# Batch 2 of each tile: probabilities turned by VectorE and reordered through DRAM in place of TensorE transposes, with a new order of all queues

## What is computed

```python
xq = q.reshape(b, s, N_KV_HEADS, N_REP, HEAD_DIM)     # 8 groups x 4 x 32
xk = k.reshape(b, t, N_KV_HEADS, HEAD_DIM)            # t = 257
xv = v.reshape(b, t, N_KV_HEADS, HEAD_DIM)
scores = einsum('bsgrd,btgd->bgrst', xq, xk) / sqrt(HEAD_DIM) + mask
probs = softmax(scores, axis=-1)
out = einsum('bgrst,btgd->bsgrd', probs, xv)

x = x + xattn(layernorm(x), ctx, ctx, 0, mask)
x = x + s4_convolution(layernorm(x), ...)
x = x + gated_experts(layernorm(x), ...)
```

## Time and profile before

| what | value |
|---|---|
| median of three timed executions | 1288.33 us (1287.66 to 1290.14) |
| the profiled execution, its own time | 1290.52 us |
| its span, first to last instruction | 1288.6 us |
| mean granted TensorE clock | 0.992 |
| TensorE busy | 1232.9 us, 96% |
| ScalarE busy | 1122.9 us, 87% |
| VectorE busy | 959.7 us, 74% |
| GpSimd busy | 825.4 us, 64% |
| DMA | 166.38 MB, share 40.9% of 16 engines for SP's queue |
| transposes of `pr` on TensorE | 2048 |

### The profile page before, as it was taken

One profiled execution on the slowest core, in us unless ns is written; L12 is line 12 of the kernel. 1 busy time (PEld: TensorE's weight loads), 2 busy tenths in 40 slices (PEclk: granted clock), 3 DMA queues, 4 the chain that ended last, 5 costly groups with the idle time before them and its releaser, 6 DMA issues.

```text
span 1288.6 us, 41515 instructions
## 1 busy us (share of the span) xinstructions
PE 1232.9 (96%) x13676; PEld 1083.1 (84%) x13676; DVE 959.7 (74%) x3424; ACT 1122.9 (87%) x3337; POOL 825.4 (64%) x1259
## 2 busy tenths in 40 slices
PE   3679999999999999999999999999999999999997
PEld 2558888888888888888888888888888888888886
DVE  6977777777777777877777777677777877877753
ACT  5889999998999999999999999989999999999841
POOL 4447676776667677666767766676777666777520
PEclk9979999999999999999999999999999999999999
DMA  7443443443344444434544433453443344444210
GB/s 237 134 127 93 151 155 122 130 133 125 119 148 152 124 130 132 129 123 141 155 122 131 147 124 118 134 154 123 131 151 123 122 128 154 132 125 132 61 60 33
DMA packets 150103, 166.38 MB, mean 129 GB/s; under 512 B 58217, under 2 KB 116082, under 8 KB 149890
## 3 DMA queue, kind: packets, MB, share of 16 engines
q1 hardware_dynamic: 149890, 163.72, 40.9%
HBM read 128.50 MB, written 34.08 MB: 126 GB/s over the span
## 4 chain that ended last, share of the span: by engine, by line
PE 76%; DVE 5%; DMA 4%; POOL 4%; ACT 4%; issue 3%; SPq 2%; DVEq 0%; ACTq 0%; POOLq 0%
PE ps_p L562 22%; PE ps_p L633 15%; PE ps_p L661 12%; PE ps_p L648 12%; PE ps_p L594 8%; PE ps_s L574 7%; ACT pr L840 2%; DMA dn<-den 2%; DMA xq<-in_x 1%; POOL lastp L1093 1%; DVE ms L1387 1%; SPq L381 1%; ACT pts L772 1%; DMA vl<-in_ctx 1%; POOL lastp L1103 1%
## 5 line engine op out<-in xcount | busy, mean ns | idle before, releaser
L840 ACT ACTIVATE pr<-ms,negmax 128x256 f32<-128x256 f32 x1024 | 512.6, 504 | 17.3 <-DVE negmax L1387 17.3
L1387 DVE CUSTOM_DVE_ANT_0 ms<-ps_s,neg_mask,last 128x256 f32<-128x256 f32 x1024 | 447.0, 473 | 7.1 <-PE ps_s L574 6.2
L772 ACT ACTIVATE pts<-ps_p 128x512 f32<-128x512 f32 x512 | 298.3, 590 | 45.8 <-PE ps_p L562 29.1
L562 PE MATMUL ps_p<-ident,pr 128*128 128x128 f32 x2048 | 296.5, 280 | 10.4 <-ACT pr L840 5.1
L562 PEld LDWEIGHTS ps_p<-ident,pr 128*128 128x128 f32 x2048 | 229.1, 142 | 48.0 <-issue 17.4
L840 ACT ACTIVATION_READ_ACCUMULATOR pr<-ms,negmax 128x1 f32 x1024 | 199.6, 195 | 0.0
L1061 POOL TENSOR_TENSOR kt<-kr,kt 128x512 fp32r<-128x512 f32 x128 | 164.9, 1288 | 24.1 <-ACT kt L772 24.1
L648 PE MATMUL ps_p<-wa_hi,ut_hi 128*128 128x288 f32 x512 | 159.6, 312 | 1.4 <-DVE ut_lo L1203 1.4
L648 PE MATMUL ps_p<-wa_lo,ut_hi 128*128 128x288 f32 x512 | 151.8, 296 | 0.0
L648 PE MATMUL ps_p<-wa_hi,ut_lo 128*128 128x288 f32 x512 | 151.7, 296 | 0.0
L1203 DVE TENSOR_TENSOR ut_lo<-ps_p,ut_hi 128x512 fp32r<-128x512 f32 x128 | 87.7, 690 | 74.8 <-ACT ut_hi L772 74.5
(11 more groups left out here) (139 smaller groups left out, 2584.6 us busy)
## 6 DMA issues: line engine op xcount, KB each, us to landing
cx<-in_ctx SPq DMA_DIRECT2D x128, 256.0 KB, 3.9
kr<-in_keys SPq DMA_DIRECT2D x128, 256.0 KB, 3.0
xq<-in_x SPq DMA_DIRECT2D x32, 512.0 KB, 4.3
turn_q<-xq SPq DMA_DIRECT2D x32, 512.0 KB, 2.9
qx<-turn_q SPq DMA_DIRECT2D x128, 128.0 KB, 2.9
xr<-in_x SPq DMA_DIRECT2D x32, 512.0 KB, 3.9
out_x<-tmp SPq DMA_DIRECT2D x32, 512.0 KB, 3.2
dn<-den SPq DMA_DIRECT2D x512, 2.0 KB, 2.3
```

What stands on the lines that cost most here:

```text
L562: mm = pe.transpose(into[:, j * P:(j + 1) * P], source, ident[:, :])
L772: return act.activation(out, in_, ACT.Copy, scale=scale)
L840: act.activation(pr[:, b % 2, g, :], ms[:, n % MS, :], ACT.Exp, bias=negmax[:, n % MS:n % MS + 1], scale=-1.0, accum_out=den[:, b, g:g + 1 ...
L1387: dve.tensor_tensor_reduce(ms[:, n % MS, :], ps_s[:, g % GPH, g // GPH * SW:(g // GPH + 1) * SW], neg_mask[:, 0:SW], 1.0, last[:, it % 2, ...
```

## The change

For batch 2 of every tile (`TURNED = (2,)`), TensorE's transposes and ScalarE's copies go. In their place:

- `exp` writes the four groups of a half of `pr` interleaved, so that element (group g, key j * 128 + i * 32 + t) stands at column ((i * 2 + j) * 4 + g) * 32 + t.
- `p_turn` (VectorE, twice for each tile, after `maximum` 23 and after `maximum` 29 and the first `q_turn`) turns half of `pr` in place, 128x1024, in 32x32 blocks: afterwards partition (r, t) holds, for each (i, j, g), the 32 positions.
- `store_p` (SP, twice) writes such a half, 512 KB, to `turn_p` in DRAM, 4 KB from each partition.
- `load_p` (SP, twice) waits for the store of its half and reads it back: partition t * 4 + i, for each r a run of 1 KB, into `pts`, 512 KB.
- `attend` for batch 2 reads its moving operand from there, as four runs of 32 columns, 512 elements apart, and waits for `p_loaded`, not for `pair_copy`.
- The host lays the context rows out as `values`, so that `load_context` brings one run of 2 KB to each partition for all batches, and for batch 2 in the key order t * 4 + i that the loaded probabilities have.
- `exp` of a batch that reuses a half of `pr` waits for `p_stored` where the one before was batch 2, and for `pt_done` otherwise, now once for each half.
- The lists of all five engines and the table `BANKS` are written anew. In the SP list of an iteration the two stores stand first, then `turn_last`, the two loads, `load_context(it - 1, 2)`, `load_residual(it - 1)`, `move_den(it - 1, 2)` and `(it - 1, 3)`.

```diff
-PAIRS = STEPS // 2
+TURNED = (2,)
+def paired(m):
+    return sum(k // GPH not in TURNED for k in range(m))
+PAIRS = paired(STEPS // 2)
+            def store_p(it, k, h):
+                sp.wait_ge(p_turned[k][h], at(it, 1, 1))
+                if at(it, 16, 0) > 0:
+                    sp.wait_ge(p_loaded[k][h], at(it, 16, 0))
+                sp.dma_start(turn_p[k, h, :, :, :],
+                             pr[:, TURNED[k] % 2, GPH * h:GPH * (h + 1), :]).then_inc(p_stored[k][h], 16)
+            def load_p(it, k, h):
+                b = TURNED[k]
+                sp.wait_ge(p_stored[k][h], at(it, 16, 16))
+                if at(it, 2 * BPT, 2 * b - 2) > 0:
+                    sp.wait_ge(pv_done, at(it, 2 * BPT, 2 * b - 2))
+                sp.dma_start(pts[:, b % 2 * GPH:(b % 2 + 1) * GPH, h * SW:(h + 1) * SW],
+                             turn_p[k, h, :, :, :].rearrange("(r t) i c -> (t i) r c", r=REP)).then_inc(p_loaded[k][h], 16)
             def attend(it, hh):
-                pe.wait_ge(pc_done, at(it, PAIRS, 2 * hh + 2))
+                if b in TURNED:
+                    pe.wait_ge(p_loaded[TURNED.index(b)][h], at(it, 16, 16))
+                else:
+                    pe.wait_ge(pc_done, at(it, PAIRS, paired(2 * hh + 2)))
+                turned = pts[:, b % 2 * GPH:(b % 2 + 1) * GPH, :].rearrange("p r (h j q s) -> p h j q r s", h=HALVES, j=TBLK, q=GPH)
...
+            def p_turn(it, k, h):
+                b = TURNED[k]
+                dve.wait_ge(e_done, at(it, STEPS, GROUPS * b + GPH * (h + 1)))
+                half = pr[:, b % 2, GPH * h:GPH * (h + 1), :].rearrange("p g c -> p (g c)")
+                dve.transpose(half, half).then_inc(p_turned[k][h], 1)
```

More of the change, by code:

```diff
@@ L67 @@
 BANKS = {
[L68 to L71, removed]
+    "pair": (1, 0, 0, 2, 0, 2, 0, 2, 2, 0, 3, 3, 0, 3, 1, 3,),
+    "out": (1, 0,),
+    "u": (0, 1,),
+    "z": (3, 1,),
     "g": (1,),
-    "y": (2, 3,),
+    "y": (0, 1,),
     "f": (3, 2,),
-    "b": (1, 0,),
+    "b": (1, 2,),
     "o": (3, 2, 3, 1,),
-    "keys": (0,),
+    "keys": (2,),
     "router": (2,),
[L79 to L83, removed]
+    "sums": (2,),
+    "dft": (3,),
+    "rows": (1,),
+    "strip": (3, 1, 2,),
+    "w": (1, 1, 2, 0, 2, 3, 2, 1, 0, 1, 3, 1, 0, 2, 3, 3,),
 }
@@ new lines, in _ @@
+            pair_chunk(31, 0); pair_chunk(31, 1); attend(30, 4); attend(30, 5); scores(31, 1); attend(30, 6)
+            attend(30, 7); pair_chunk(31, 2); experts(29, 0, 0, 1); experts(29, 0, 1, 3); experts(29, 0, 3, 5)
+            out_chunk(30, 0); out_chunk(30, 1); experts(29, 0, 5, 6); experts(29, 0, 6, 8); pair_chunk(31, 3)
+            pair_chunk(31, 4); gated_chunk(29); scores(31, 2); attend(31, 0); attend(31, 1); pair_chunk(31, 5)
+            pair_chunk(31, 6); expand(29, 0, 0, 4); expand(29, 1, 0, 2); expand(29, 1, 2, 3); expand(29, 1, 3, 4)
@@ new lines, in _ @@
+            u_chunk(30, 0); scores(31, 3); pair_chunk(31, 7); u_chunk(30, 1); convolve(30, 0, 0, 4)
+            convolve(30, 1, 0, 1); convolve(30, 1, 1, 8); z_chunk(30, 0, 0); attend(31, 2); z_chunk(30, 1, 0)
+            attend(31, 3); pair_chunk(31, 12); pair_chunk(31, 13); pair_chunk(31, 14); experts(30, 1, 0, 1)
+            experts(30, 1, 1, 3); pair_chunk(31, 15); experts(30, 1, 3, 4); experts(30, 1, 4, 6); experts(30, 1, 6, 8)
+            attend(31, 4); attend(31, 5); attend(31, 6); attend(31, 7); experts(30, 0, 0, 1); experts(30, 0, 1, 3)
@@ new lines, in _ @@
+            q_stats(2, 2); q_turn(1, 1); maximum(0, 24); weight_low(4, 1); maximum(0, 25); p_turn(0, 0, 1)
+            maximum(0, 26); maximum(0, 27); maximum(0, 28); maximum(0, 29); maximum(0, 30); weight_low(5, 0)
+            maximum(0, 31); s4_step(); weight_low(5, 1); s4_step(); maximum(1, 0); maximum(1, 1); s4_step()
+            maximum(1, 2); maximum(1, 3); s4_step(); maximum(1, 4); weight_low(6, 0); maximum(1, 5); maximum(1, 6)
+            maximum(1, 7); normalisers(0); weight_low(6, 1); maximum(1, 8); maximum(1, 9); maximum(1, 10)
@@ new lines, in _ @@
+            maximum(1, 11); maximum(1, 12); weight_low(7, 0); maximum(1, 13); maximum(1, 14); maximum(1, 15)
+            out_half(0, 0); out_half(0, 1); weight_low(7, 1); maximum(1, 16); maximum(1, 17); u_stats(0, 0)
+            u_stats(0, 1); maximum(1, 18); u_stats(0, 2); maximum(1, 19); maximum(1, 20); maximum(1, 21)
+            maximum(1, 22); maximum(1, 23); strip_low(0); strip_low(1); strip_low(2); q_turn(2, 0); u_low(0, 0)
+            maximum(1, 24); u_low(0, 1); maximum(1, 25); maximum(1, 26); maximum(1, 27); p_turn(1, 0, 0)
@@ new lines, in _ @@
+            maximum(31, 17); maximum(31, 18); u_stats(30, 1); u_stats(30, 2); maximum(31, 19); maximum(31, 20)
+            maximum(31, 21); third_residual(29, 0, 1); p_turn(31, 0, 0); maximum(31, 22); maximum(31, 23)
+            third_residual(29, 1, 1); u_low(30, 0); maximum(31, 24); u_low(30, 1); maximum(31, 25); maximum(31, 26)
+            maximum(31, 27); p_turn(31, 0, 1); second_residual(30, 0, 0); maximum(31, 28); maximum(31, 29)
+            z_stats(30, 0, 0); maximum(31, 30); second_residual(30, 1, 0); maximum(31, 31); z_low(30, 0); z_low(30, 1)
```

513 lines of the change are left out of this document (253 added, 260 removed).

## The result

| | before | after |
|---|---|---|
| median of the timed executions | 1287.99 us (1280.84 to 1290.14) | 1246.03 us (1243.65 to 1252.40) |
| profiled execution, its own time | 1290.52 us | 1252.40 us |
| its span | 1288.6 us | 1250.6 us |
| ratio of the mean times | | 0.9691, interval 0.9665 to 0.9716 |

The change makes the kernel 3.1% faster by the means of the timed executions (3.3% by the medians in the table). The first rows are busy time by stretch (stretch, length, busy us of PE, PEld, DVE, ACT, POOL, then granted clock, DMA share, GB/s) of the kernel after, beside the earlier trace rows; the third covers some 25 periods, and the second fence has the same stretch of before.

What follows compares the result with a forecast made beforehand. TensorE was taken to bound the kernel, at 37.57 us per iteration. Profiled 1290.5 - 52.8 (chunks) + 6 (hand-overs) + 2 (tail) = 1245.7; with the median 2.2 lower, 1243.5, say 1244, range 1229 to 1274.

Steps and rivals of the forecast that it cites:

- The saving per tile: TensorE gives up batch 2's four pair chunks of transposes, 0.44 us each: 1.76 us a tile, 52.8 us over 30 tiles.
- rival (b): Larger gain on TensorE: joined chunks and the dearer chunk price save 2.1 us a tile, 63 in all, 1227; chance 0.14.
- The new operations: Block transpose 1.2 us on VectorE, 512 KB store landing in 2.9 and load in 5, exponentials and attends at no extra cost.
- (c): Batch 2's strided moving operand doubles two attends a tile on TensorE, +1.0 us; 17 us saved, 1273; chance 0.05.
- The layout of the iteration: New order priced from the start of scores: TensorE's list sums to 35.1 us, convolve at 26.2, next scores at 35.2.
- The cover of 0.2 us: Before convolve on TensorE: VectorE's u_low(0) ends at 26.0 us, wanted at 26.2; the tightest hand-over found.
- The cover of 2.2 us at the attend: Before attend(it, 4): batch 2's context, queued behind the probabilities' load, lands at 39.5 us, 2.2 before the attend at 41.7.
- The allowance for hand-overs: TensorE waits at convolve's u_low and the attend's loads: 0.2 us a tile, 6 us given back over 30 tiles.
- The head: First 90 us, bound by loads, ScalarE and VectorE: removed TensorE work gains 0, with 5 us either way for the order.
- The tail: End of the run pays the trip through DRAM once, +2 us, as only some of tile 30's experts precede attend(31, 4).
- the signs that I had named: If right: TensorE above 98% busy, period near 35.9, 1536 pr transposes, VectorE 86%, ScalarE 90%, pts loads within 6 us.
- (d): Trip through DRAM holds TensorE before attend, a loss once the load lands 9.4 us after issue: 1300 or more; chance 0.08.

Runs made afterwards that it cites:

- the kernel without the trip: Changed kernel with the two stores and two loads of batch 2's probabilities doing nothing, so part of the output isn't computed: 1230.08 us, ratio 0.9550 to the kernel before.

## Why the prediction was right, and where it wasn't

The mechanism was right: TensorE sets the pace, and the removed chunks are what is gained. That the time came out at 1246.0 for a forecast of 1244 is in part luck. In the profiled execution, against the forecast's terms, the period gave 5 us less for the chunks and 13 us less for hand-overs, and head and tail gave 8 and 3 us more; besides, this execution was 6 us above the median.

- **The saving per tile** was taken as 4 x 0.44 = 1.76 us. It measures 1.64 by TensorE's work in after and 1.65 by the kernel without the trip. Right within 0.12, and the 0.12 is the new order's: with the chunks put back into that order their price is 1.77. The dearer price of 1.87, and with it rival (b), was not.
- **The new operations**: 1.2 us, landing in 5 and 2.9 us, exponentials and attends unchanged. Measured 1.22, 4.8, 3.2, 501 against 504 ns, 276 against 277 ns. All right, and (c) falls.
- **The layout of the iteration** holds nearly to the tenth. From `scores(it, 0)` at 579.71 of the trace of after, `u_low(0)` is ready at 26.1 (forecast 26.0) and `convolve` starts at 26.3 (26.2). The next `scores` start at 35.7 (35.2), as late as the 0.6 us by which the old sum had been short would suggest. The cover of 0.2 us that I called the tightest is there, and it suffices:

```profile
605.14 0.68 DVE L1238 TENSOR_TENSOR ut_lo<-ps_p,ut_hi 128x512 fp32r<-128x512 f32 x1
```

```profile
579.71 0.98 PE L607 MATMUL ps_s<-kt,qs 32*128 32x256 f32 x24
...
606.00 0.48 PE L671 MATMUL ps_p<-strip_hi,ut_hi 128*128 128x512 f32 x1
```

- **The cover of 2.2 us at the attend** was mis-sized. The loads go out 0.6 later than laid out (34.6, not 34.0). The context was to land 0.5 us behind the loads, at 39.5; it was issued at 615.26, 35.6, and the attend had it at 622.45, 42.7. That is 7.2 us after issue, where I had gone by the median of 3.9. The median of all context loads is still 3.6; this one stands behind 1 MB of loads. Over the 29 tiles in which it directly follows them it lands after 5.2 us in the median and 4.8 to 7.1 in all, so it is in time as a rule, and the attend waits for it in 8 tiles. The trace of before had given 7.1 as the longest, and that was the row to use for a transfer at the end of a burst.
- **The allowance for hand-overs**, 0.2 us a tile or 6 us, measured 0.65, or 19, of which the pair chunks' wait for `exp` is 0.46 and the context 0.13. The step that failed is the search for what is late next: I laid out the trip's own two deadlines, and not those of what stands behind it in SyncE's queue. I had noted that residual and denominators stand there, gave them a late deadline, and left out `store(it - 3)`, whose landing GpSimd needs, with `last_exp(it, 1)`, `exp` 13 and pair chunk 6 behind. Moving `last_exp` shortened the period by 0.27, and `gated_low` on top by 0.13 (one profiled execution each; only the two together are clear of noise in time).
- **The two rules of the Trainium skill.** The load of the probabilities, 512 KB in runs of 1 KB, lands in 4.8 us and the store in 3.2, so nothing of a strided DMA's slowness is seen here. By the Trainium skill, "VectorE: DVE Perf Modes", section "The three transpose paths", it shouldn't be, since its warning is for a large innermost stride; the trace agrees. Its factor of 19 no run here tests. The kernel without TensorE's transposes of batch 2 is 3.1% faster. "Rules for kernel authors" on the same page of the Trainium skill would have left them with TensorE; where TensorE is the engine that is full, the measurement decides against it.
- **The head** was taken as 0, with 5 either way. It gives 8.0 us, and TensorE is busy 62.3 of the first 100 us, not 58.8. Its origin isn't settled. In the new order with the batch 2 chunks put back, the first product of experts comes at 121.7 against 105.8 with the turn, so the removed work counts in the head as well; but the old lists with the turn give 115.3 against 113.9 of before, so the order counts too.
- **The tail** was to cost 2 and gave 1.1.
- The sum: 29 x (1.64 - 0.64) + 8.0 + 1.1 = 38.1, against the forecast's 52.8 - 6 - 2 = 44.8 on the same scale; the rest of the agreement in the median is that the profiled execution of after was 6.4 us above its median, where that of before was 2.5.
- Of the signs that I had named, TensorE above 98% between 200 and 1100 us is just missed (97.9). The period of 35.9 isn't met by after (36.50), but by the kernel without the trip. ScalarE was to be at 90% and is at 89, VectorE at 86 is at 86. The 1536 transposes are there; the loads of `pts` land in 4.8 us in the median, the longest in 7.0, over the 6 that I had named. The context is the transfer that the attends wait for (3.7 us in 8 times, against 0.3 once for the probabilities), as (d) was to show itself, at a small part of its price.

## What to carry to other kernels

When a kernel's full engine is relieved by a detour over DMA, the detour's own two legs are easily laid out, and they held here to some tenths. What has to be laid out as well is each entry that shares the issuing queue behind them, with the buffer whose release hangs on its landing, and with the landing time of a transfer in a burst, not the median. Moving one entry of a crowded queue forward moves the lateness to its neighbours: three of the four such moves tried here made the kernel slower than it had been. Moving the waiting instruction on its compute engine, behind work that needn't wait, took the waits away; by itself its gain in time was within noise, and with a second such move it was clear.

## What the runs showed of the hardware

- An in-place block transpose of 128x1024 fp32 by VectorE takes 1.22 us, against 0.70 for 128x512, 13% less than two of the smaller would take (2 x 0.70 = 1.40).
- The same 512 KB store of x lands 3.8 us (median) after issue at the end of the burst and 7.7 us in the middle of it, with a DMA share of about 0.6 in both kernels. A mean share says nothing of such a place.
- A moving operand in four runs of 32 fp32 columns, 2 KB apart, costs TensorE nothing (276 ns for batch 2 against 275 to 278 for the others; two attends take 1.01 us to the next row, 622.45 to 623.46, as before), and an exponential that writes runs of 32 is as fast as one that writes 256 in one run (500 ns against 500 to 504).
- A 256 KB load issued right behind 1 MB of loads lands 5.2 us after issue in the median and up to 7.1, where the median of all loads of its kind is 3.6.
